# Reordering the start-up of a fused attention and feed-forward kernel: row maxima, roundings and low halves of the first two batches

## The reference

```
xn  = layernorm(x)
S   = (xn * w_lhs) @ (xn * w_rhs)^T          # 512 x 512
att = softmax(S) @ xn                        # 512 x 128
x1  = x + layernorm(att)
h   = silu(x1n @ W1 * s1) * (x1n @ W2 * s2)  # x1n = layernorm(x1), 512 hidden
h   = gelu(h @ H1 * sh1)
h   = gelu(h @ H2 * sh2)
out = x1 + layernorm(h @ W3 * s3)
```

## Time and profile before

| what | value |
|---|---|
| median of 3 runs | 496.38 us (496.02 to 496.4) |
| the profiled execution | 496.54 us, its span 494.8 us |
| TensorE matmul busy | 477.8 us, 97% of the span |
| ScalarE busy | 450.2 us, 91% |
| VectorE busy | 395.8 us, 80% |
| GpSimd busy | 235.1 us, 48% |
| mean granted TensorE clock | 0.996 of full speed |

### The profile page before, as it was taken

How to read it: one execution, slowest core, us unless ns; L and a number is a source line. 1 busy time by engine, 2 the same in 40 slices (tenths; PEclk the granted TensorE clock), 3 DMA queues, 4 the chain that set the end, 5 groups by cost and what they waited for, 6 DMA issues and landing times.

```text
span 494.8 us, 9479 instructions
## 1 busy us (share of the span) xinstructions
PE 477.8 (97%) x2850; PEld 388.7 (79%) x2850; DVE 395.8 (80%) x1179; ACT 450.2 (91%) x780; POOL 235.1 (48%) x257
## 2 busy tenths in 40 slices
PE   7789999999999999999999999999999999999994
PEld 6567788888888888888888888888888888888783
DVE  5999889796987969689696978969596878757565
ACT  4799999999999999999999999999999899996963
POOL 4475764635254563534556254463705434463531
PEclk9999999999999999999999999999999999999998
DMA  8022002110203011020301103020030020310012
GB/s 288 32 66 85 2 15 72 43 43 7 101 0 106 0 48 58 1 105 0 106 0 42 64 0 106 1 95 33 1 86 1 0 87 0 87 44 1 1 44 88
DMA packets 12845, 24.23 MB, mean 49 GB/s; under 512 B 1552, under 2 KB 2064, under 8 KB 12816
## 3 DMA queue, kind: packets, MB, share of 16 engines
q1 hardware_dynamic: 12816, 23.87, 14.8%
HBM read 15.48 MB, written 8.39 MB: 48 GB/s over the span
## 4 chain that ended last, share of the span: by engine, by line
PE 86%; DVE 6%; ACT 2%; issue 1%; POOL 0%; DVEq 0%; ACTq 0%; POOLq 0%
PE hid_bank L377 23%; PE hid_bank L379 23%; PE score_bank L313 5%; PE hid_bank L398 3%; PE hid_bank L402 3%; PE hid_bank L403 3%; PE hid_bank L399 3%; PE w_bank L377 3%; PE w_bank L379 3%; PE mix_bank L363 3%; PE w_bank L322 2%; PE mix_bank L367 2%; PE mix_bank L364 2%; PE score_bank L345 2%; PE score_bank L351 2%; PE score_bank L348 2%
## 5 line engine op out<-in xcount | busy, mean ns | idle before, releaser
L377 PE MATMUL hid_bank<-hA_hi,w_hi 128*128 128x512 f32 x256 | 106.3, 415 | 0.1
L377 PE MATMUL hid_bank<-hB_hi,w_hi 128*128 128x512 f32 x256 | 103.8, 405 | 0.0
L379 PE MATMUL hid_bank<-hA_lo,w_hi 128*128 128x512 f32 x256 | 101.3, 396 | 0.0
L379 PE MATMUL hid_bank<-hB_lo,w_hi 128*128 128x512 f32 x256 | 101.1, 395 | 0.0
L2233 POOL TENSOR_TENSOR hC_lo<-hC_full,hC_hi 128x512 fp32r<-128x512 f32 x60 | 76.9, 1296 | 19.2 <-ACT hC_full L1230 19.0
L1180 ACT ACT_TABLE_LOAD x51 | 65.4, 1283 | 1.6 <-PEq L2409 0.7
L1591 DVE SCALAR_TENSOR_TENSOR hA_full<-hid_bank,columns,gate 128x512 f32<-128x512 f32 x64 | 47.4, 748 | 16.4 <-ACT gate L1223 15.8
L379 PEld LDWEIGHTS hid_bank<-hB_lo,w_hi 128*128 128x128 f32 x256 | 48.3, 189 | 10.1 <-DVE hB_lo L1742 0.4
L377 PEld LDWEIGHTS hid_bank<-hB_hi,w_hi 128*128 128x128 f32 x256 | 48.2, 188 | 9.9 <-DVE hB_lo L1742 0.2
L379 PEld LDWEIGHTS hid_bank<-hA_lo,w_hi 128*128 128x128 f32 x256 | 48.4, 189 | 8.9 <-DVE hA_lo L1738 0.3
L377 PEld LDWEIGHTS hid_bank<-hA_hi,w_hi 128*128 128x128 f32 x256 | 48.3, 188 | 9.1 <-DVE hA_full L1591 0.5
(11 more groups left out here) (147 smaller groups left out, 1203.6 us busy)
## 6 DMA issues: line engine op xcount, KB each, us to landing
x_res<-x_dram SPq DMA_DIRECT2D x16, 256.0 KB, 2.7
out_dram<-x SPq DMA_DIRECT2D x16, 256.0 KB, 2.0
x_tail<-out_dram SPq DMA_DIRECT2D x16, 256.0 KB, 2.7
out_dram<-y_out SPq DMA_DIRECT2D x15, 256.0 KB, 3.0
x_in<-x_dram SPq DMA_DIRECT2D x14, 256.0 KB, 2.8
w_raw<-weights_dram SPq DMA_DIRECT2D x5, 512.0 KB, 6.7
x_in<-x_dram SPq DMA_DIRECT2D x2, 128.0 KB, 2.2
x_ahead<-x_dram SPq DMA_DIRECT2D x1, 256.0 KB, 3.1
```

The source lines that it names most:

```text
L377: nc.tensor.matmul(bank[:, :], w_hi[:, w], hi, start=first, stop=False)
L379: mm = nc.tensor.matmul(bank[:, :], w_hi[:, w], lo, start=False, stop=last and not general)
```

## The change

The change moves instructions inside the `start()` functions and adds one helper; it leaves the loop and `finish()` as they are. TensorE: `attend(0, 0)` comes after all four `turn_e(0, j)`. ScalarE: `sum_lo(0)` goes ahead of `softmax(0, 0)`, `softmax(0, 2)` ahead of `high_e(0, 0)`, `sum_lo(2)` ahead of `softmax(1, 0)`; the rounding of the second batch's `xn` to `xn_hi` comes to ScalarE (`high_second_xn`), between `sum_lo(1)` and `sum_lo(3)`; `high_weights(1)` leaves ScalarE. VectorE: the four `row_max(0, j)` stand together ahead of `x_statistics(2)`; `high_xn(1)` goes; `low_aT(1)` and `low_aT(2)` each move ahead of the statistics before them; `row_max(1, 0)` and `row_max(1, 1)` are mixed with `aggregate(ln_att, 0)`. GpSimd: `high_weights(1)` is added behind `high_weights(2)`.

```diff
 # TensorE, start()
                 turn_e(0, 1)
-                attend(0, 0)
                 turn_e(0, 2)
                 turn_e(0, 3)
+                attend(0, 0)
 # ScalarE
+            def high_second_xn():
+                act.wait_ge(xn_ready, 2)
+                act.wait_ge(pv_done, T)
+                nc.scalar.copy(xn_hi[:, :, :], xn[:, :, :]).then_inc(xn_hi_ready, 1)
 ...
                 high_weights(0)
+                sum_lo(0)
                 softmax(0, 0)
-                sum_lo(0)
                 softmax(0, 1)
+                softmax(0, 2)
                 high_e(0, 0)
-                softmax(0, 2)
                 softmax(0, 3)
 ...
                 sum_lo(1)
+                high_second_xn()
                 sum_lo(3)
+                sum_lo(2)
                 softmax(1, 0)
 ...
                 high_e(1, 2)
-                sum_lo(2)
                 sum_lo(5)
                 sum_lo(4)
-                high_weights(1)
                 high_e(1, 3)
 # VectorE, start()
                 row_max(0, 1)
-                x_statistics(2)
                 row_max(0, 2)
                 row_max(0, 3)
+                x_statistics(2)
                 low_e(0, 0)
 ...
                 low_xT(1)
-                high_xn(1)
+                low_aT(1)
                 attention_statistics(0)
-                low_aT(1)
+                row_max(1, 0)
                 aggregate(ln_att, 0)
+                row_max(1, 1)
                 normalize_x(2, 0)
-                row_max(1, 0)
-                row_max(1, 1)
 ...
                 low_xT(2)
+                low_aT(2)
                 x1_statistics(0)
-                low_aT(2)
                 aggregate(ln_x1, 0)
 # GpSimd, start()
                 high_weights(2)
+                high_weights(1)
                 high_weights(5)
```

## The result

The changed kernel takes 501.18 us (median of 4 runs, 500.96 to 501.63) against 496.39 us for the kernel before (4 runs, 496.02 to 497.33): a ratio of 1.0095, 95% interval 1.0077 to 1.0112. It is 4.8 us slower. The forecast was 499.2 us with a range of 497.0 to 500.1: the sign was right, the size was not.

The account below looks back on a forecast made before the run. VectorE's queue was taken to set the pace up to 60 us, with TensorE full behind it. A gain of 1.14 us and 4.0 us of held normalisations summed to +2.9 us: 499.2 us on the 496.38 us median, range 497.0 to 500.1.

Parts of the forecast that it names:

- which wait is removed and what follows: GpSimd near 31 us: low_weights(1) no longer waits for ScalarE's w_hi, starts 0.30 us ahead of the first normalisation.
- the pattern of the holds: First x1 normalisations on VectorE: two GpSimd low halves hold the first and second, the last ends 4.0 us later.
- Rival 1: The port is passed only once: the four normalisations follow the first GpSimd instruction, +1.9, sum +0.75, 497.1 us; chance 0.08.
- the sum: Whole kernel: VectorE's queue gain of -1.14 plus +4.0 us for the held normalisations, +2.9 us, giving 499.2 us.
- the gain of VectorE's queue: VectorE up to aggregate(ln_x1, 0), at 29.48 in the old trace: 0.54 + 0.42 + 0.18 = 1.14 us earlier.
- GpSimd's casts of weights at 14.63 and 15.19 wait for a transfer and don't move: Start, batch 1: the casts still hold the normalisations, so normalize_x(1, 3) starts at 16.27 instead of 16.81, gain 0.54.
- The row maxima in the gap: VectorE's 1.21 us idle before 12.70: row_max(0, 2) and (0, 3) fill it, normalize_x(1, 0) comes 1.1 us ahead.
- `aT_lo` of the second batch: TensorE, waiting 1.42 us for it at 21.77, gets it 1.76 us earlier; forecast near 19.2.
- the free place of GpSimd's added cast: The 1.04 us cast of high_weights(1) lies in GpSimd's 2.34 us wait before 14.63, so costs nothing there.
- A shift of VectorE's queue before 60 us is passed on one to one: Up to 60 us VectorE sets the pace; behind it both engines are full, without gaps in which to catch up.
- rival 4: The reorder does nothing: only the held normalisations remain, up to 500.2 us; chance 0.06, with other slower cases.
- rival 3: rs_eps at 49.13 slips ahead of GpSimd and is no longer held: 2.2 us return, 497.0 us; chance 0.05.

Follow-up runs that it names:

- experiment 4: The changed kernel with one GpSimd wait added, so low_weights(1) starts only after the four x2n of the first batch: 495.64 us, ratio 0.9989 to the kernel before.
- experiment 2: The kernel before with only high_weights(1) moved from ScalarE to GpSimd, behind high_weights(2): 502.18 us, ratio 1.0116.
- experiment 3: The kernel before with only sum_lo(2) moved ahead of softmax(1, 0) on ScalarE: 501.61 us, ratio 1.0109.
- experiment 7: The changed kernel with a GpSimd wait between low_weights(1) and low_weights(4) until the four x2n are written: 498.52 us, ratio 1.005 to the kernel before.
- experiment 9: The kernel before with one GpSimd wait added, so low_weights(0) starts only after rs_eps (scaled_eps(2)): 495.6 us, ratio 0.9985.
- experiments 4 to 8: Five runs on the changed kernel; the one not named singly adds 20 and 14 unread TensorE products around the first turn_x2 tile: 502.16 us.
- experiment 8: The changed kernel with GpSimd waits putting low_weights(1) behind the four x2n and low_weights(0) behind rs_eps: 495.01 us, ratio 0.9975 to the kernel before.
- Experiment 6: The changed kernel with unread TensorE products, 10 ahead of the first turn_x2 and 8 behind its first tile: 498.99 us, ratio 1.0057 to the kernel before.
- experiment 1: The changed kernel with high_weights(1) put back on ScalarE behind sum_lo(4): 501.17 us, ratio 1.0094 to the kernel before.

## Why the prediction was right in its sign and wrong in its size

**Right: which wait is removed and what follows.** The earlier trace rows of before showed GpSimd idle for 1.15 us until `w_hi`, with the four normalisations inside this gap. That the idle time of an engine off the critical path was what kept two others apart is shown by experiment 4, which restores the order and nothing else, and by experiments 2 and 3, which take it away from the old kernel.

**Right: the pattern of the holds.** Forecast were a first `x2n` of some 2.2 us, a second of 2.3 to 2.6, two of 0.34. Measured: 2.13, 2.38, 0.34, 0.34. Rival 1, a single hold, is out; experiment 7 shows what it would have looked like. The Trainium skill ("SBUF — State Buffer", section "Who interferes with whom") says that the first to issue holds the shared ports for the whole instruction; the trace agrees, with each held `x2n` ending some 0.1 us behind a GpSimd instruction. The hold came to 3.84 us (2.39 + 1.45), for which the sum had 4.0.

**Nearly right: the gain of VectorE's queue.** The sum had 1.14 us at `aggregate(ln_x1, 0)`, the trace has 1.45, of which 0.14 is an earlier first transfer (first statistics at 2.84 instead of 2.98 us). One pair of traces doesn't measure this gain to better than about 1 us: on the instructions of the kernel before the aggregate comes at 29.48 and, in experiment 9, at 28.82 us; on those of the change (changed kernel, experiments 4 to 8) at 27.96 to 28.99 us. The means, 29.15 and 28.23, are 0.9 us apart. These rows, of VectorE and of GpSimd, answer to the earlier trace rows:

```profile
14.03 1.76 DVE L1758 TENSOR_SCALAR xn<-x_ahead,ln_x_mean_var,ln_x_rstd 128x128 f32<-128x128 f32 x3
...
15.78 0.34 DVE L1758 TENSOR_SCALAR xn<-x_ahead,ln_x_mean_var,ln_x_rstd 128x128 f32<-128x128 f32 x1
...
18.69 0.74 DVE L1651 SCALAR_TENSOR_TENSOR aT_lo<-w_bank,neg_wlr,aT_hi 128x512 fp32r<-128x512 f32 x1
```

```profile
13.85 1.60 POOL L2255 CAST w_hi<-w_raw 128x512 fp32r<-128x512 f32 x2 [0.74 <-DMA w_raw<-weights_dram]
```

"GpSimd's casts of weights at 14.63 and 15.19 wait for a transfer and don't move" did not hold in this trace: the transfer landed 0.8 us earlier, and the casts with it. The change need not be the cause: with the instructions of the kernel before the casts start at 13.96 us in experiment 9, and with the changed ones at 14.80 in experiment 8. The normalisations were caught all the same (three take 1.76 us where three free ones take about 0.9), but they were let go earlier, and `normalize_x(1, 3)` starts at 15.78, not at 16.27. The row maxima in the gap, `aT_lo` of the second batch at 18.69 (forecast 19.2), and the free place of GpSimd's added cast, in what was its wait before 14.63, came out as reasoned. ScalarE's `high_second_xn` took 0.62 us at 18.80, and VectorE shows no idle time behind it until 27.9 us.

**Wrong: "A shift of VectorE's queue before 60 us is passed on one to one".** This is the step that failed. The forecast counted the hold as a delay of VectorE and asked only how much later each engine starts. It did not ask what TensorE does while it waits. TensorE idled 2.56 and 1.76 us, the granted clock fell to half, and what it owed behind the wait (three turns, two attends, `turn_e(2, 0)`) then took 1.6 us longer on the path to `high_e(2, 0)`. With this term the sum is -1.45 + 3.84 + 1.6 = +4.0 us, and the trace has 3.95. Experiment 6 removes the term and keeps the hold; experiment 7 keeps the term and removes nearly all the hold; each comes out at its own part of the sum. So the forecast missed by about 2.0 us: 1.6 for the clock, less 0.5 for a gain larger and a hold shorter than in the sum, plus 0.8 for the end of the span and the lie of the medians. The 0.5 is in part luck of the two starts.

The range had a slip of its own. With the gain lost and the hold of 4.0 us kept, the prediction's terms give 500.4 us, not the 500.2 of rival 4, and a gain of 0.8 us gives 499.6, not 500.0; the stated upper end, 500.1, leaves rival 4 outside. The measured 501.18 lies above all of them.

**Wrong: the price of rival 3.** It said that "2.2 us return" if `rs_eps` is not held. Experiments 8 and 9 put it at 0.7 in the traces. The reading of the earlier trace rows that VectorE sets the pace because it is busy 10.00 of 10 us passed over TensorE's 9.88 beside it. Two full engines leave to one of them only what the other has spare. The hold is also counted as busy time: of the 2.34 us of `rs_eps` from 49.13 us on, nearly 1.5 lie inside VectorE's 10.00 us and are no work.

**Incomplete: who guarded the gap.** The prediction named `high_weights(1)` alone. Experiment 1 showed that returning it does not restore the gap, and experiment 3 that `sum_lo(2)` guards it as well. For the forecast this changed nothing, since both moved.

**Open.** Experiment 4 gains less by its median (0.6 us) than its profiled execution promises (1.1 to 1.3 us), which took 495.16 us, 0.5 below the median; for experiment 8 the two are 1.0 and 1.15 us. The start differs between executions: the aggregate of `ln_x1` comes at 28.33 us in experiment 4 and at 28.99 in 8, on the same instructions up to there. One difference stands in the traces. In experiment 8 TensorE's first score products take some 0.80 us, in the changed kernel 0.50:

```profile
9.51 0.80 PE L348 MATMUL hid_bank<-xT_lo,aT_hi 128*128 128x512 f32 x1
```

In experiment 4 the first two take 0.78 and 0.79 us. That looks like half clock at the start, though the granted clock of these windows reads 1.00, so it is an estimate from the durations. It does not set the start alone: in experiment 9 the first one takes 0.78 us as well, and its aggregate comes earlier than in the kernel before. How much of the rest is the arrival of the first transfers, and how often either happens, was not tried.

## What to carry to other kernels

Before an instruction is moved off an engine, look at who waits for it and what runs while they wait: an idle gap of an engine off the critical path can be the only thing that keeps it from VectorE's normalisations. Where such an order matters, write it as a wait; here one line was worth 5.5 us on the changed kernel (5.3 by the ratios).

A delay of the engine that feeds TensorE has two prices: its length, and what TensorE loses at half clock afterwards. Read the granted clock around every idle time of a microsecond or more that the forecast creates, above all where several stand close together (in experiment 2 it fell with waits of 1.28 and 1.91 us), and give it a term of its own.

If two engines are both full in a stretch, removing a stall on one returns only what the other has left, and a busy share near 1 may itself be made of held instructions: compare the count of instructions, not the busy time.

## What the runs showed of the hardware

Between queued instructions of VectorE and GpSimd that hold each other up, the turn changes hands: with `low_weights(1)` under way and `(4)` queued behind it, one normalisation got in between the two (2.13 to 2.27 us, then 2.38 or 2.39 us for the next), in all six traces in which they collided. Two normalisations never got in. Not every GpSimd instruction holds VectorE: beside a root of GpSimd (92.07 to 93.08 us in the kernel before) a normalisation at 92.16 us took its usual 0.34 us.

TensorE's clock did not fall in the waits of 0.77 us for `x2n`, nor in single waits of 1.42 us (21.77 us in the kernel before) and 1.76 us (25.52 us in the changed one). With a wait of 2.56 us it fell to 1.2 GHz within that wait in the changed kernel, in the second one in experiment 1, and in experiment 7 only when TensorE was at work again (33.1 us, with 1.00 in the window before). So the same wait was followed by the fall at different distances, which the forecast could not place, and the half clock outlasts the wait: it was still there 2.9 us (experiment 3) to 6.1 us (experiment 2) after the last wait had ended. The Trainium skill ("TensorE: Matmul & The Clock Gate", section "What's actually happening") has the gate set by how busy the engine was recently, with half and full speed as its only levels; the granted clocks of 0.50 and 1.00 agree. Products that nothing reads, put into the wait, kept it at 2.4 GHz: 18 of them made the kernel 1.9 (by the ratios) to 2.2 us faster.
